# A feature-crossing recommender kernel: eight field pairs copied by DMA over both partition halves, five spread on TensorE, one dense turn

## The reference

```python
emb = tables[feat_idx, sparse]                      # (2048, 26, 32)
linear_out = lin_sparse_w[feat_idx, sparse].sum(-1) + dense @ lin_dense_w
x0 = xk = emb
for w, bb in ((conv1_w, conv1_b), (conv2_w, conv2_b)):   # 128 outputs each
    hp = einsum('bhd,bmd->bhmd', xk, x0).reshape(-1, h * M, E)
    xn = sigmoid(einsum('oi,bid->bod', w, hp) + bb[None, :, None])
    xk = xn[:, :64]; res.append(xn[:, 64:])
cin_out = (concat(res, 1).sum(-1) @ cin_w + cin_b)[:, 0]
h3 = tanh(tanh(tanh(deep_x @ W1 + b1) @ W2 + b2) @ W3 + b3)   # 845 -> 1024 -> 512 -> 256
return linear_out + cin_out + (h3 @ deep_w + deep_b)[:, 0] + bias[0]
```

## Time and profile before

| what | value |
|---|---|
| median of 3 runs | 1629.52 us (1625.16 to 1629.81) |
| profiled execution | 1624.22 us, its span 1622.4 us |
| TensorE busy (matmuls) | 1543.6 us, 95% of the span |
| VectorE, ScalarE, GpSimd busy | 1104.7, 643.5, 709.2 us |
| largest groups of TensorE | y from xb (L751) 436.0, xn (L745) 369.7, y from hp (L751) 366.0 |
| chain of waits | TensorE 86%, issue 4%, VectorE 3%, DMA 1% |
| DMA | 319.80 MB, mean 197 GB/s; SyncE's queue 75.0% of 16 engines' time |

### The profile page before, as it was taken

The page is one execution under the profiler, slowest core; times in us unless marked ns, Lnnn a source line. Parts: engine busy times, 40 slices in busy tenths (PEclk is TensorE's granted clock), DMA queues, the critical chain, the costliest instruction groups (busy, mean ns, idle before and its releaser), DMA issues.

```text
span 1622.4 us, 23599 instructions
## 1 busy us (share of the span) xinstructions
PE 1543.6 (95%) x6584; PEld 656.8 (40%) x6584; DVE 1104.7 (68%) x1017; ACT 643.5 (40%) x904; POOL 709.2 (44%) x600
## 2 busy tenths in 40 slices
PE   0598999999999999999999999999999999999999
PEld 0232333333333333333333333333333336787876
DVE  3276777777777877787777777787877783333332
ACT  2342434344434443434443434434343323344443
POOL 7356565556555556565555646464731110000000
PEclk9899999999999999999999999999999999999999
DMA  6688999999999999999998989898999884634531
GB/s 126 143 183 194 231 214 223 217 231 209 226 212 225 211 224 209 221 214 229 210 228 200 232 201 231 201 240 201 237 203 235 204 210 122 186 120 147 175 104 53
DMA packets 178599, 319.80 MB, mean 197 GB/s; under 512 B 31132, under 2 KB 106812, under 8 KB 178524
## 3 DMA queue, kind: packets, MB, share of 16 engines
q1 hardware_dynamic: 155423, 298.87, 75.0%
q10 hardware_dynamic: 9828, 13.43, 4.1%
q0 software_dynamic: 13312, 7.06, 3.8%
HBM read 297.93 MB, written 21.31 MB: 197 GB/s over the span
## 4 chain that ended last, share of the span: by engine, by line
PE 86%; issue 4%; DVE 3%; another core or an unknown queue 2%; POOL 2%; DMA 1%; SPq 1%; ACT 1%; ACTq 0%; DVEq 0%; POOLq 0%
PE y L751 42%; PE xn L745 19%; PE bc L880 16%; PE bc L731 5%; PE bc L738 3%; DVE hp L692 2%; POOL emb L542 2%; PE bc L723 1%; DVE xb L692 1%; SPq L465 1%; DMA x0t<-x_halves 1%; DMA x_lo<-dense_halves 0%; ACTq L370 0%; DMA emb<-table,idx_stage 0%
## 5 line engine op out<-in xcount | busy, mean ns | idle before, releaser
L692 DVE TENSOR_TENSOR hp<-bc,xk 128x1024 f32<-128x1024 f32 x384 | 453.9, 1219 | 271.3 <-PE bc L731 136.0
L542 POOL DMA_INDIRECT emb<-table,idx_stage x416 | 515.9, 1240 | 145.5 <-issue 126.3
L692 DVE TENSOR_TENSOR xb<-xb,xk 128x1024 f32<-128x1024 f32 x448 | 546.5, 1264 | 27.9 <-ACT xk L927 23.9
L751 PE MATMUL y<-xb,w2s 128*64 128x512 f32 x1792 | 436.0, 601 | 0.0
L745 PE MATMUL xn<-sq,w1s 128*128 128x512 f32 x768 | 369.7, 618 | 4.4 <-issue 4.4
L751 PE MATMUL y<-hp,w2s 128*64 128x512 f32 x1536 | 366.0, 597 | 0.0
L553 POOL TENSOR_TENSOR r<-r 128x512 f32<-128x512 f32 x96 | 123.5, 1287 | 351.0 <-ACT r L932 181.3
L926 ACT ACTIVATE xk<-xn,bias 64x512 f32<-64x512 f32 x128 | 87.4, 683 | 438.5 <-PE xn L745 248.8
L922 ACT ACTIVATE sq<-bc 128x1024 f32<-128x1024 f32 x192 | 182.9, 1026 | 197.5 <-PE bc L738 145.8
L751 PEld LDWEIGHTS y<-xb,w2s 128*64 128x64 f32 x1792 | 116.0, 136 | 248.8 <-issue 201.5
L745 PEld LDWEIGHTS xn<-sq,w1s 128*128 128x128 f32 x768 | 137.5, 192 | 162.6 <-issue 154.8
(11 more groups left out here) (57 smaller groups left out, 843.3 us busy)
## 6 DMA issues: line engine op xcount, KB each, us to landing
xb<-x_rows SPq DMA_DIRECT2D x896, 256.0 KB
w_raw<-W SPq DMA_DIRECT2D x32, 448.0 KB
x0t<-x_halves ACTq DMA_DIRECT2D x252, 52.0 KB
x_halves<-deep_halves SPq DMA_DIRECT2D x30, 384.0 KB
w_raw<-W SPq DMA_DIRECT2D x16, 512.0 KB
emb<-table,idx_stage POOLq DMA_INDIRECT x416
x_hi<-x_halves SPq DMA_DIRECT2D x24, 256.0 KB
x_lo<-x_halves SPq DMA_DIRECT2D x24, 256.0 KB
```

Source lines behind the costliest of these rows:

```text
L542: nc.gpsimd.indirect_dma_start(out=emb[:, m, :], out_offset=None, in_=table, in_offset=bass.IndirectOffsetOnAxis(ap=idx_stage[:, m:m + 1], ...
L692: nc.vector.tensor_tensor(product(n)[:, :], x[:, :], xk[sl % 2][:, :], ALU.mult).then_inc(multiplied, 1)
L751: last = nc.tensor.matmul(y2[H * c:H * c + H, :], w2s[:, ORDER[n], :], src[:, c * CHUNK:(c + 1) * CHUNK], start=(n == 0), stop=(n == PAIRS ...
```

## The change

Eight pairs are copied and five are spread by TensorE (3, 4, 5, 9, 10; the fill of three, then of two). Copies are five groups, `COPIED`: (0), (1, 2), (6, 7), (8), (11, 12); a group of two is copied together. The pair's second field now stands on partitions 32 to 95 and the first on 0 to 31 and 96 to 127, so each group takes three transfers, and waits for the contraction of its last pair. The order of TensorE's step is: K fill; products 8 to 12 of the last step, with the dense turn between them in step 1, now all seven transposes in one slot; fill of 3, 4, 5; both halves of `contract_k` one after the other, in two PSUM banks that alternate with the step and take turns with y2's; fill of 9, 10; products 0 to 7. The products wait for the read of the first half, in whose bank they accumulate. The turn is in step 1 in tile 0 too, which gathers all 26 rows for it in one run. `dump_halves` stays behind the copy i == 2 of step 2, which is now the group (6, 7). The linear terms move to the end of the last step.

```diff
-PAIR_ROWS = ((0, slice(0, H)), (1, slice(H, P)))
+QUARTER = P // 4
+
+PAIR_ROWS = ((1, slice(QUARTER, 3 * QUARTER)), (0, slice(0, QUARTER)), (0, slice(3 * QUARTER, P)))
 
 
 def second_of_pair(p):
-    return p // H
+    return int(QUARTER <= p < 3 * QUARTER)
...
-ORDER = [0, 1, 2, 3, 8, 4, 5, 9, 6, 7, 10, 11, 12]
-BY_PE = (3, 4, 6, 7, 9, 10)
+ORDER = [0, 1, 2, 3, 8, 4, 5, 6, 9, 10, 7, 11, 12]
+BY_PE = (3, 4, 5, 9, 10)
 assert sorted(ORDER) == list(range(PAIRS))
-BY_DMA = tuple(n for n in range(PAIRS) if n not in BY_PE)
+COPIED = ((0,), (1, 2), (6, 7), (8,), (11, 12))
+BY_DMA = tuple(n for ns in COPIED for n in ns)
+assert sorted(BY_PE + BY_DMA) == list(range(PAIRS))
...
 STEP_WORK = (
     ("fill", (("K", 0), ("K", 1), ("K", 2))),
     ("of_last", (8, 9, 10)),
-    ("fill", (("D", 0), ("D", 1), ("D", 2))),
+    ("fill", (("D", 0),)),
     ("of_last", (11, 12)),
-    ("fill", (3, 4)),
+    ("fill", (3, 4, 5)),
     ("first", 0),
-    ("of_this", (0, 1, 2)),
-    ("fill", (6, 7)),
     ("first", 1),
     ("fill", (9, 10)),
-    ("of_this", (3, 4, 5, 6, 7)),
+    ("of_this", (0, 1, 2, 3, 4, 5, 6, 7)),
 )
 LEFT = tuple(n for kind, what in STEP_WORK if kind == "of_last" for n in what)
 DEEP_PARTS = range(0, 3), range(3, KD - 1), range(KD - 1, KD)
+
+TURNS = ((0, 1, 2),)
...
-def deep_step(ahead):
-
-    return 2 if ahead == 3 else 1
+
+DEEP_STEP = 1
...
-        dense_lo = [hp[4 + i][0:ND, :].bitcast(F32R) for i in range(2)]
+        dense_lo = [x[0:ND, :].bitcast(F32R) for x in (hp[4], xb[7])]
...
-        xn = pb("xn", [P, CHUNK])
-        y2 = pb("y2", [P, CHUNK])
+
+        acc = [pb(f"acc{i}", [P, CHUNK]) for i in range(2)]
+        terms = acc[(STEPS - 2) % 2]
...
+        def first_acc(sl, c):
+            return acc[(sl + c) % 2]
...
-            tile(0, True, 3)
+            tile(0, True, 2)
...
             def spread_by_dma(t, sl, i):
+                ns = COPIED[i]
+                at = BY_DMA.index(ns[0])
+                fields = x0_rows[bass.ds(t, 1), :, :].rearrange("t (m e) b -> t m e b", e=ROW)
                 for f, parts in PAIR_ROWS:
-                    first = (2 * ORDER[BY_DMA[i]] + f) * ROW + sl * STEP_D
-                    row = x0_rows[bass.ds(t, 1), first:first + STEP_D, :].rearrange("t d b -> t (d b)")
-                    sp.dma_start(xb[i][parts, :], row.to_broadcast([parts.stop - parts.start, COLS])).then_inc(spread[i], 16)
+                    first, last = (2 * ORDER[n] + f for n in (ns[0], ns[-1]))
+                    rows = fields[:, first:last + 1:max(last - first, 1), sl * STEP_D:(sl + 1) * STEP_D, :]
+                    rows = rows.rearrange("t m d b -> t m (d b)").to_broadcast([parts.stop - parts.start, len(ns), COLS])
+                    dst = xb_all[parts, at * COLS:(at + len(ns)) * COLS].rearrange("p (m c) -> p m c", c=COLS)
+                    sp.dma_start(dst, rows).then_inc(spread[i], 16)
 
             def tile(t, is_first, ahead):
                 for sl in range(STEPS):
                     s = t * STEPS + sl
-                    for i, n in enumerate(BY_DMA):
+                    for i, ns in enumerate(COPIED):
                         if not (is_first and sl == 0):
-                            sp.wait_ge(contracted, contracted_by(s - 1, n))
+                            sp.wait_ge(contracted, contracted_by(s - 1, ns[-1]))
                             hold()
                         spread_by_dma(t, sl, i)
-                        if i == 2 and sl == 2 and not is_first and ahead > 0:
+                        if i == 2 and sl == DEEP_STEP + 1 and ahead > 0:
                             dump_halves(t + 1)
-                    if sl == 2 and is_first:
-                        dump_halves(t + 1)
-                    if sl == deep_step(ahead) and ahead > 0:
+                    if sl == DEEP_STEP and ahead > 0:
...
+            sp.wait_ge(dense_dumped, 64)
...
-                    gather(range(PAIRS), gathered)
+                    gather(range(M), gathered)
...
-                            i = BY_DMA.index(n)
-                            dve.wait_ge(spread[i], s * (16 * len(PAIR_ROWS)) + 16 * len(PAIR_ROWS))
-                            x = xb[i]
+                            for i, ns in enumerate(COPIED):
+                                if n == ns[0]:
+                                    dve.wait_ge(spread[i], s * (16 * len(PAIR_ROWS)) + 16 * len(PAIR_ROWS))
+                            x = xb[BY_DMA.index(n)]
...
-                    turn_deep(slot, DEEP_PARTS[use[1]])
+                    turn_deep(slot, [k for part in TURNS[use[1]] for k in DEEP_PARTS[part]])
...
-            contract_k(0)
-            pe.wait_ge(xn_read, 1)
-            contract_k(1)
+            for c in range(2):
+                contract_k(c, first_acc(-1, c))
...
                         elif kind == "of_last" and not start:
                             for n in what:
                                 pe.wait_ge(multiplied, multiplied_by(s - 1, n))
-                                contract(n)
-                            if final and what[-1] == PAIRS - 1:
-                                pe.wait_ge(xn_read, ALL_STEPS * 2)
-                                pe.wait_ge(end_loaded, END_LOADED)
-                                pe.wait_ge(lin_done, TILES)
-                                add_term(cwd[:, :], dense_rows, start=True)
-                                add_linear()
+                                contract(n, acc[(sl - 1) % 2])
                         elif kind == "of_this":
-                            if what[0] == 0 and not start:
-                                pe.wait_ge(y2_read, s)
+                            if what[0] == 0:
+                                pe.wait_ge(xn_read, s * 2 + (2 if final else 3))
                             for n in what:
                                 pe.wait_ge(multiplied, multiplied_by(s, n))
-                                contract(n)
+                                contract(n, acc[sl % 2])
                         elif kind == "first" and not final:
                             if what == 0:
                                 pe.wait_ge(squared, squared_by(s, K1 - 1))
-                            pe.wait_ge(xn_read, s * 2 + (2 + what))
-                            contract_k(what)
+                            if what == 0:
+                                pe.wait_ge(xn_read, s * 2 + 2)
+                            elif not start:
+                                pe.wait_ge(y2_read, s)
+                            contract_k(what, first_acc(sl, what))
                     if final:
+                        pe.wait_ge(y2_read, s)
+                        pe.wait_ge(end_loaded, END_LOADED)
+                        pe.wait_ge(lin_done, TILES)
+                        add_term(cwd[:, :], dense_rows, start=True)
+                        add_linear()
                         pe.wait_ge(r1_step, TILES * SUMS)
                         add_term(cw1[:, :], sum1)
                         for n in LEFT:
                             pe.wait_ge(multiplied, multiplied_by(s, n))
-                            contract(n)
+                            contract(n, acc[sl % 2])
...
-            def turned_deep(slot, part):
+            def turned_deep(slot, part, first_k):
                 ks = DEEP_PARTS[part]
                 rows = rows_of(ks)
-                src = bc[slot][rows, 0:len(ks) * P].rearrange("p (k b) -> p k b", b=P)
+                at = (ks[0] - first_k) * P
+                src = bc[slot][rows, at:at + len(ks) * P].rearrange("p (k b) -> p k b", b=P)
...
+                xn = first_acc(sl - 1, c)
...
-                nc.scalar.activation(r2[:, sl, :], y2[:, :], ACT.Sigmoid, bias=bias2[:, :]).then_inc(y2_read, 1)
+                nc.scalar.activation(r2[:, sl, :], acc[sl % 2][:, :], ACT.Sigmoid, bias=bias2[:, :]).then_inc(y2_read, 1)
...
-                            late = is_first and sl == 2
-                            if what == int(late) and (sl < 2 or ahead > 0):
+                            if what == 0 and (sl < 2 or ahead > 0):
```

More of the change, by code:

```diff
@@ L93, in step_fills @@
         fills = [use for use in fills if not is_k(use)]
[L94 removed]
+    if ahead == 0 or sl != DEEP_STEP:
         fills = [use for use in fills if not is_d(use)]
@@ L112, in group_of @@
     return int(2 * ORDER[n] >= PER_GROUP)
-assert all(group_of(BY_PE[i]) != group_of(BY_PE[i + 1]) for i in range(0, len(BY_PE), 2))
+assert all(group_of(n) != group_of(n + 1) for n in BY_PE if n + 1 in BY_PE)
 def fill_at(sl, use, ahead):
@@ L277, in build @@
         dumped = sem("dumped")
-        spread = [sem(f"spread{i}") for i in range(len(BY_DMA))]
+        spread = [sem(f"spread{i}") for i in range(len(COPIED))]
         filled = sem("filled")
@@ L802, in add_term @@
                 for g in range(GROUPS):
-                    last = nc.tensor.matmul(xn[32 * g:32 * g + 1, 0:CHUNK], w, x[:, g * CHUNK:(g + 1) * CHUNK],
```

(8 more changed lines are left out.)

50 lines of the change are left out of this document (19 added, 31 removed).

## The result

| what | before | after |
|---|---|---|
| median | 1628.97 us (1625.16 to 1629.81, 4 runs) | 1727.04 us (1712.65 to 1732.33, 4 runs) |
| profiled execution, span | 1624.22, 1622.4 us | 1723.9, 1722.1 us |
| DMA | 319.80 MB | 353.34 MB |

What follows compares the result with a forecast made beforehand. The prediction took TensorE's own work to bound the kernel, with DMA nearly full at 0.95. Gains of 54 us and a new wait of 54 us cancelled, giving 1629 us against a median of 1629.52, range 1598 to 1680.

Steps and rivals of the forecast that it cites:

- The regular step: TensorE's plain step without waits: 18.80 us instead of 19.35, 0.55 less.
- The dense turn: Seven transposes in step 1 of each tile: would cost 1.07 us, as before.
- The wait in step 2: Eight products wait for ScalarE's read behind the dump of the halves: 3.6 us a tile (1.6 to 5.6), 54 in all.
- if older copies still fill the queue: Upper bound within the wait in step 2: ScalarE starts its loads at 11.5 us of the step instead of 9.5.
- rival (e): Clock falls to its lower level in the new wait: 2.3 us a tile, 35 more, 1664 us; chance 0.12.
- A copy is issued nearer its use: cost at nothing: Copies released later in the step, covered by VectorE's idle time: nothing; without cover 1 to 3 us a step.
- The DMA floor: Copies across both partition halves at 255 GB/s: 75 us a tile, barely hidden under TensorE; bounds 65.4 and 84.4.
- rival (d): DMA becomes the bound, copies staying at 223 to 240 GB/s, floor past 79 us a tile: 1650 to 1710; chance 0.16.
- Tile 0: Dense rows turned a step earlier, so step 3's wait goes: 12.2 us gained with the four shorter steps.
- the turn comes at 91: In tile 0, 26 gathers in one run end at 78 us, hidden before the turn at 66 + 20 + 5 = 91.
- The -54: Sum of gains: 38 us in 14 tiles, 1.6 in tile 15, 12.2 in tile 0, 2.2 in the first contraction.
- The stated condition: Forecast is wrong if step 2's gap times 15 differs from the regular steps' gain by over 13 us.

Runs made afterwards that it cites:

- run 14: Kernel after with the halves written behind copy (0) and pairs 6, 7, 8 copied in the first step only: 1608.60 us, ratio 0.9942 to the kernel before.
- run 15: Kernel after with the halves written behind copy (1,2) and pairs 6, 7, 8 copied in the first step only: 1591.41 us, ratio 0.9840 to the kernel before.
- run 1: Kernel after with the write of the halves two copies earlier, behind copy (0) of step 2: 1643.52 us, ratio 1.0110 to the kernel before.
- run 6: Kernel after with the halves written behind copy (0) and each field on its own half of the partitions: 1707.44 us, ratio 1.0502 to the kernel before.
- run 2: Kernel after with each field on its own half of the partitions again, write left in place: 1806.81 us, ratio 1.1092 to the kernel before.
- run 5: Kernel after with the halves written behind copy (0) and every pair copied by its own transfers: 1637.70 us, ratio 1.0056 to the kernel before.
- run 10: Kernel after with the halves written behind copy (1,2) and every pair copied by itself: 1648.04 us, ratio 1.0141 to the kernel before.
- run 11: Kernel before with only the pairs' rows laid across both partition halves, seven pairs copied: 1620.91 us beside 1626.39, ratio 0.9972.
- run 16: The same program as run 1, all eight pairs copied, measured again in the set of run 15: 1637.65 us beside 1617.13, ratio 1.0136.
- run 13: Kernel after with the halves written behind copy (0) and pair 8 copied in the first step only: 1620.49 us, ratio 1.0006 to the kernel before.
- run 7: Kernel after with the halves written early, seven pairs copied and six spread on TensorE, in three fills: 1679.76 us, ratio 1.0317 to the kernel before.

## Why the prediction was wrong, point by point

**The regular step** was right: 18.80 predicted, 18.80 measured, in step 3 of nearly every tile and in all plain steps once nothing waits (runs 14, 15). The single fill of three pairs takes 0.66 (634.06 to 634.72), the middle that was chosen. The dense turn costs 1.40 to 1.48 more than a plain step (run 14, nearly all tiles) and not 1.07, since TensorE waits 0.34 for ScalarE's rounded copies ("ACT deep_halves" is the releaser): 5 us in all.

**The wait in step 2: mechanism right, size wrong, and this is the step that failed.** The term was 3.6 us a tile, 54 in all, between 1.6 and 5.6. Measured: 5.75 of gaps on the mean of tiles 1 to 14, and a step 8.07 longer than the plain one, so 113 us over 14 tiles, and 6 in tile 0. That the read's place behind the write is the mechanism, run 1 shows: the same write two copies earlier takes step 2 from 26.87 to 21.19. Two things were mis-sized, and a third followed.
- ScalarE's loads start at 12.5 of the step, not 9.5. The sum let (6,7) be read from 1.5 on an empty queue. VectorE's row for that step says [2.41 <-DMA xb<-x_rows] at 632.10: the copies (1,2) land only at 3.4. From there the forecast's own figures, 4.1 for 1 MB and 3.9 for the write with its end (5.6 to 9.5), give 11.4; the last 1.1 to 12.5 was not taken apart. I had put this case at the upper bound, "if older copies still fill the queue", and should have taken it, as the share of 0.95 in the earlier trace rows suggested.
- The clock: rival (e), given 0.12, came true in the same gap. It cost 1.5 us in the step shown; on the mean, 2.3 of the 8.07 are not in the gaps, and the slow products are the only other loss seen there. It was made a case of its own, though the wait that was forecast was already longer than the 3.33 of the earlier trace rows, behind which the earlier trace rows have 0.50. It should have been part of the term.
- The wait stops the release of copies, so VectorE waits in turn, 4.08 us at 653.66 for the first copy of the next step. Step 3 is 18.80 all the same, so in this kernel that wait is absorbed.

**"A copy is issued nearer its use: cost at nothing"** was wrong, and the same sentence had the right price, 1 to 3 us a step without cover. With the write early, it is 1.13 and 0.97 in step 2 (run 14) with room on the queue, and 0.4 to 1.9 in several steps without. The cover named there, VectorE idle until 5.5 of the next step, holds while (1,2) land before that; they land at 6.5 when 0.86 MB stand ahead.

**The DMA floor.** 255 GB/s was taken for the mix and 243 at a share of 1.00 were measured, so the floor is 19.4 / 0.243 = 80 us a tile and not 75. Run 1's tile is 80.3. That is rival (d), "decides once the floor passes 79", given 0.16 and hidden at first behind the longer wait. The direction of the term was right: without the crossing the rate is 229 at a share of 1.04 (run 6), and the kernel 80 us slower (run 2). The Trainium skill (SBUF — State Buffer, Door 1: The DMA port swizzle) gives 218 for one side; the estimate for this mix that the prediction worked out from its 218 and 435 was 290. On one side, 220 at a full share (229 at 1.04) agrees. For the mix the measurement decides: 243 in run 1, with two pairs a transfer (238 to 248 in the others, GB/s over share), and with one pair 242 in run 5 (240 at 0.99), 255 in run 10 (242 at 0.95) and 264 in run 11 (219 at 0.83).

**Tile 0** was to gain 12.2 us. In the kernel after it took 98.6 from its first K fill to tile 1's (60.21 to 158.82) against 91.4 before. Its steps 2 and 3 are together 7.5 shorter, the long step 2 included, but step 0 is 13.9 longer, and why is open (run 16). In run 16, with the short wait in the first step, it took 86.7, and there the turn waited 3.04 us for the gathers: "the turn comes at 91" adds 20 and 5 to the 66 at which tile 0 begins before; here tile 0 begins at 60.75, the turn is wanted at 85, and the 26 gathers, some of which took 1.8 to 1.97 instead of 0.95, are issued until 80.4 and have landed at 88.5.

**The sum.** The forecast had -54 and +54. Held against it by stretches of the two profiled executions, which differ by 99.7 us: tiles 1 to 14 are 92.3 longer where 12.1 was forecast, 62.6 of the excess in step 2 and 17.6 in steps 0 and 1; tile 0 is 7.2 longer where 8.6 shorter was forecast; tile 15 with the dense layers is 6.4 longer for 1.6 shorter, not taken apart; what lies ahead of tile 0 is 6.1 shorter for 2.2. By the runs: the write's place was worth 84 (run 1), 30 more than the term. The -54 did not come: with TensorE's wait for the read gone (0.1 us in all of run 1), the kernel stands at +13 to +20 against before. With runs 13 to 16: 29 us are bytes, 17 the write ahead of (1,2), and run 15 without either is 26 below the kernel before. Of the 28 it still lacks, 15 are its tile of 77.4 against 76.3, 14 times; the rest lies in tile 0 and the prologue and was not taken apart. The stated condition, wrong if the gap times 15 differs from the gain by over 13 us, was met with 86 and more against 38. What was not foreseen is that the two rivals on the slow side are not alternatives: the wait, the clock and the full queue came together, and each sum took only one.

## What to carry to other kernels

Where a queue runs through its program in order, a transfer tied by position ("behind the third copy") moves when the list before it changes; ask of each such tie what it now stands behind and who is behind its arrival in turn, and don't price its landing on an empty queue where the share is as high as the 0.95 here. A longer wait of TensorE is to be priced with the slow clock behind it and with the copies that can't be released meanwhile, in one sum and not as rivals. And a part can be good while the change is bad: the crossing alone on the kernel before was the one variant with all of the computation that won. One cure was not tried: ScalarE's read ahead of its four loads, so that it does not stand behind the write at all.

## What the runs showed of the hardware that was not expected

- Rows written to partitions 32 to 95 beside rows on 0 to 31 and 96 to 127 move the same 219 GB/s at a DMA share of 0.83 instead of 0.95 (run 11), though each transfer covers 32 or 64 partitions and none all 128.
- In three of five sets ScalarE's squares in the very first step came up to 4.2 us apart for no reason in the trace; the kernel before was 10 us slower in those sets as well.
- In run 7 SyncE's first copy behind its loop's jump came up to 4 us later than elsewhere in 8 of 12 tiles; with seven copied pairs that kernel was slower than the one with eight (1679.76 against 1643.52 us). The cause is open.
